# Rotary features: the exchanged halves come from the features by a product with a 0/1 matrix, instead of a second projection of the tokens

## The chip, the cores and the metric

The kernel runs on one core of a Trainium2 chip. A core has five engines with a queue each: TensorE (matrix products into PSUM, called PE in the profile; its weight loads are PEld), VectorE (DVE), ScalarE (ACT), GpSimd (POOL) and SyncE (SP, which here only issues transfers). Engines wait for each other through semaphores. The metric is the device time of one launch in microseconds, the median of three runs.

## What is computed

A tensor of 2 x 2048 tokens with 256 features goes through two layers. Layer 0 is a layer norm, a linear recurrence and a sign-weight projection. Layer 1 is a layer norm, then an ALiBi attention beside a block with RMS norm, rotary attention (16 query heads, 4 key/value heads of 16) and a mixture of 8 experts, 2 of them per token. The change touches how the rotary queries and keys are made:

```python
qkv = jnp.einsum('bsh,oh->bso', h, wqkv)          # h: RMS norm of the tokens
q = qkv[..., :NH * HD].reshape(B, S, NH, HD)      # 256 features
k = qkv[..., NH * HD:(NH + NKV) * HD]...          # 64 features
def _apply_rope(t, cos, sin):
    t1, t2 = jnp.split(t, 2, axis=-1)
    rot = jnp.concatenate([-t2, t1], axis=-1)     # halves of each head exchanged
    return t * cos[None, :, None, :] + rot * sin[None, :, None, :]
```

## The kernel before

The program has five stages in turn: `front` (layer norm and the recurrence's input), `middle` (projections), `attention` (both attentions), `after` (output projections and routing) and `experts`. The change is in `middle`; its weights are loaded in `front`, on SyncE's queue, and all transfers of weights are waited for by one count (`NW`).

`middle` works on eight blocks of 512 tokens (`NBLK = 8`, `BT = 512`), features on the partitions. Each engine has its own fixed list of work per block, the function `both(blk, more, ahead)`; `more` says that a next block exists, `ahead` that the block after next exists. Work on three blocks overlaps: in block blk, TensorE projects blk's tokens, turns u, xn and h of blk + 1 between them, and makes the first products (recurrence output with `c_mat`, sign weights) of blk + 2 (`first_products`).

TensorE's order in a block is: features 0 and 1 (ALiBi queries, from xT with `wa`), the turn of u, features 2 and 3 (keys), values 4 and 5, features 6 and 7, the turn of xn, features 8 and 9, the turn of h, features 10 and 11, the first products of blk + 2, values 12. Groups 6 to 12 come from hT with `wb`. `wb` holds the rotary weights, and beside them the same weights with the halves of each head exchanged: group 6 is query features 0 to 127, 7 the same with halves exchanged, 8 and 9 the other 128, 10 and 11 the 64 key features. A feature group is two accumulating products (the 256 inputs in two parts) into a PSUM bank; the banks 6, 7, 4, 5 go round (`BANK`). Products here are in float32 and appear as two records each. The turns are transposes with the identity matrix, eight records each.

ScalarE's order is: `scale_ffn(blk + 1)`, high parts 0 and 1, `deviation`, high parts 2 and 3, `squares(blk + 1)` (four sums of squares of xn, L704), `take_xT(blk + 1)` (two copies from PSUM and a small square root, L710 and L712), high parts 4 and 5 (L738), `take_hT(blk + 1)` (L717), high part 6. A high part is the result rounded to the narrower format that the attention reads; VectorE then forms the low part (L839), the rest.

VectorE's order is: `form_u(blk + 1)`, low parts 0 and 1, `add_residual`, low parts 2 and 3, `normalise` (makes xn), the values' bias, `mean_square(blk + 1)` (L813, waits for squares), `rope(4)`, `form_h(blk + 1)` (L817 and L820, waits for take_xT's square root), `rope(5)`, low parts 4 and 5, `rope(6)`, low part 6, and the copy of the rotary values (L889). `rope(m)` multiplies the group by cos (L850), its exchanged twin by sin (L851), and adds (L854).

The waits that tie them: the turn of h waits for `form_h`; `first_products(blk + 2)` waits until `take_xT` and `take_hT` of blk + 1 have emptied their banks; the next block's first features wait for the copy at L889.

Of the kernel before, what the change touches and what calls it, by code (L numbers as in the profile page):

```python
# [14 lines left out]
P = 128  # L15
# [3 lines left out]
TPB = 4  # L19
# [26 lines left out]
FT = FFN // P  # L46
SCALE = HD ** -0.5


# [22 lines left out]
def front(nc, A, M):  # L72
# [5 lines left out]
    with ExitStack() as ctx:  # L78
# [37 lines left out]
        s_aug, s_augr = sem("front_aug_loaded_then_stored"), sem("front_aug_rounded")  # L116
        x_d = A["x"].rearrange("b (n p) d -> p (b n) d", p=P)
        block = ctx.enter_context(nc.Block())

# [5 lines left out]
        def _(sp):  # L125
# [8 lines left out]
            for dst, src in ((M["wa"][:, :, :], A["w_qkv"].rearrange("(k p) m -> p k m", p=P)),  # L134
                             (M["bv"][:, :], A["b_qkv"][2 * D:3 * D].partition_broadcast(P)),
                             (M["wb"][:, :, :], A["w_b"].rearrange("(k p) m -> p k m", p=P)),
                             (M["cos"][:, :], A["c_cos"]), (M["sin"][:, :], A["c_sin"])):
                sp.dma_start(dst, src).then_inc(M["s_mid_weights"], 16)
# [249 lines left out]
def middle_weights(nc, ctx, M):  # L388

    for name, shape in (("c_mat", [P, D]), ("w_raw", [P, KD, D]), ("wa", [P, KD, 3 * D]), ("ba", [P, 4]),  # L390
                        ("bv", [P, D]), ("wb", [P, KD, 2 * D + 3 * KV * HD]), ("cos", [P, L]), ("sin", [P, L]),

                        ("cols", [P, KD, 4])):
        M[name] = ctx.enter_context(nc.sbuf_tensor("m_" + name, shape, F32))
    M["s_mid_weights"] = nc.alloc_semaphore("mid_weights_loaded")
    M["s_signs"], M["s_signed"] = nc.alloc_semaphore("signs_loaded"), nc.alloc_semaphore("signs_ready")
# [30 lines left out]
def middle(nc, A, M):  # L427

    with ExitStack() as ctx:
        def sb(name, shape, dt=F32):  # L430
            return ctx.enter_context(nc.sbuf_tensor(name, shape, dt))

        def sem(name):
            return nc.alloc_semaphore(name)
# [24 lines left out]
        NS = 7  # L459
        xf = [sb(f"m_xf{i}", [P, BT]) for i in range(2)]  # L460
        rots = [sb(f"m_rot{i}", [P, BT]) for i in range(2)]
# [12 lines left out]
        s_hi, s_xf, s_lo = sem("mid_high_part"), sem("mid_rope_ready"), sem("mid_low_part")  # L474
        s_va = sem("mid_v_ready")
        s_st = [sem(f"mid_rows_stored{s}") for s in range(2)]
# [7 lines left out]
        vb_d = M["vb_d"].rearrange("(n p) c -> p n c", p=P)  # L484
        NW = 10
        NDVE = 6
# [91 lines left out]
        def _(pe):  # L578
# [39 lines left out]
            def features(n, w, at, m, src):  # L618
# [4 lines left out]
                ins.then_inc(s_pr, 1)  # L623

            def values(n, w, at, m, src, tiles):

# [16 lines left out]
            def both(blk, more, ahead):  # L643
# [17 lines left out]
                pe.wait_ge(s_lo, blk * NS + 4)  # L661
                features(7, wb, D, P, hT)
                if more:
                    turn_xn(blk + 1)
                pe.wait_ge(s_pd, blk * NDVE + 2)
                features(8, wb, P, P, hT)
                pe.wait_ge(s_pd, blk * NDVE + 3)
                features(9, wb, D + P, P, hT)
                if more:
                    turn_h(blk + 1)  # L670
                pe.wait_ge(s_pd, blk * NDVE + 4)
                features(10, wb, 2 * D, KV * HD, hT)
                features(11, wb, 2 * D + KV * HD, KV * HD, hT)
                if ahead:
# [3 lines left out]
                    first_products(blk + 2)  # L678
                pe.wait_ge(s_pd, blk * NDVE + 5)
                values(12, wb, 2 * D + 2 * KV * HD, KV * HD, hT, range(TPB))  # L680

# [5 lines left out]
        def _(act):  # L687
# [36 lines left out]
            def both(blk, more, ahead):  # L724

                def high(m):
# [10 lines left out]
                    else:  # L737
                        sc.activation(part[m][0:n, 0, :], xf[(blk % 2 * NS + m) % 2][0:n, :], ACT.Copy).then_inc(s_hi, 1)  # L738

# [6 lines left out]
                high(2)  # L746
                high(3)
                if more:
                    squares(blk + 1)
                    take_xT(blk + 1)  # L750
                high(4)
                high(5)
# [7 lines left out]
        def _(dve):  # L760
# [66 lines left out]
            def both(blk, more, ahead):  # L827
                tok = blk % NBB * BT

                def low(m):  # L830
# [7 lines left out]
                    else:  # L838
                        ins = v.tensor_tensor(part[m][0:n, 1, :], xf[(blk % 2 * NS + m) % 2][0:n, :], high, ALU.subtract)  # L839
                    ins.then_inc(s_lo, 1)  # L840

                def rope(m):

                    rot = rots[m % 2]
                    i = (blk % 2 * NS + m) % 2
                    n = P if m < 6 else KV * HD
                    a, r = (6, 8, 10)[m - 4], (7, 9, 11)[m - 4]
                    dve.wait_ge(s_lo, blk * NS + (4 if m < 6 else 5))
                    dve.wait_ge(s_pr, blk * 13 + (r + 1))
                    ch.did(v.tensor_tensor(xf[i][0:n, :], ps[BANK[a % 4]][0:n, :], cos[0:n, tok:tok + BT], ALU.mult))  # L850
                    v.tensor_tensor(rot[0:n, :], ps[BANK[r % 4]][0:n, :], sin[0:n, tok:tok + BT],  # L851
# [1404 lines left out]
def constants():  # L2256
# [17 lines left out]
    ang = (np.arange(L, dtype=np.float32)[:, None] * inv[None, :]).astype(np.float32)  # L2274
    emb = np.concatenate([ang, ang], axis=1).T
    sign = np.where(np.arange(HD) < HD // 2, -1.0, 1.0).astype(np.float32)[:, None]
    c["c_cos"] = np.tile(np.cos(emb), (P // HD, 1)).astype(np.float32)
# [49 lines left out]
```

## Time and profile before

| | |
|---|---|
| median of 3 runs | 2570.25 us (2568.62 to 2571.12) |
| the profiled execution | 2568.78 us, with a span of 2566.9 us |
| TensorE busy | 2326.3 us, 91% of the span |
| VectorE, ScalarE, GpSimd busy | 1917.9, 1516.4 and 579.8 us |
| mean granted clock of TensorE | 0.964 |
| middle stage, from its first feature product to its last copy | 137.4 to 378.8 us |

The span is from the first to the last instruction. Busy time counts instructions of an engine; TensorE's products are pipelined, so that the length of one record is more than the distance to the next, and costs are better read from how far groups of records stand apart. The granted clock is a share of full speed: 1.00 is 2.4 GHz, 0.50 is 1.2 GHz.

### The profile page before, as it was taken

What the parts mean: (1) busy time and instruction counts of PE and PEld (TensorE: products, weight loads), DVE (VectorE), ACT (ScalarE), POOL (GpSimd) and SP (SyncE); (2) the same over time, 40 slices, a digit from 0 to 9 for tenths busy, and PEclk for the clock granted to TensorE, in tenths of its full rate; (3) what the DMA queues carried; (4) which work ended last, traced back from release to release, by engine and by line L of the source; (5) the groups of instructions that cost most, each with busy time, mean ns of one, the idle gap of its engine ahead of it and who ended that gap; (6) DMA issues with size and microseconds to landing.
All of it is one profiled execution on the core that took longest, in us unless ns stands there. A gap on an engine that the chain in (4) does not pass through costs nothing. (4 is left out here: it accounts for less than half of the span.)

```text
span 2566.9 us, 52951 instructions
## 1 busy us (share of the span) xinstructions
PE 2326.3 (91%) x18274; PEld 1266.1 (49%) x18275; DVE 1917.9 (75%) x4030; ACT 1516.4 (59%) x3290; POOL 579.8 (23%) x845
## 2 busy tenths in 40 slices
PE   3299987999999999999999999999999883999997
PEld 2155544444444444444444444444443662788886
DVE  6767758988998998999998999998993573233332
ACT  2033323677777787777787777777778461222221
POOL 4412101121111111111111111111000266423223
PEclk9599997999999999999999999999999996999999
DMA  4157766553443443322322322322020894343433
GB/s 156 62 161 207 222 193 98 86 104 76 72 77 73 78 78 67 70 56 46 66 54 52 64 53 55 63 48 61 31 78 26 284 299 186 64 77 76 78 74 70
DMA packets 168302, 246.55 MB, mean 96 GB/s; under 512 B 52392, under 2 KB 125240, under 8 KB 162244
## 3 DMA queue, kind: packets, MB, share of 16 engines
q0 software_dynamic: 38304, 112.51, 23.2%
q1 hardware_dynamic: 122404, 120.68, 15.9%
q10 hardware_dynamic: 7380, 10.48, 1.4%
q8 instruction: 138, 2.26, 0.4%
q14 instruction: 76, 0.62, 0.1%
HBM read 120.19 MB, written 122.36 MB: 94 GB/s over the span
## 5 line engine op out<-in xcount | busy, mean ns | idle before, releaser
L1411 DVE TENSOR_REDUCE a_mx<-banks 128x1 f32<-128x512 f32 (+3 forms) x2560 | 1378.5, 603 | 127.3 <-PE banks L1240 58.8
L1371 ACT ACTIVATE a_p<-banks 128x512 f32<-128x512 f32 (+3 forms) x2560 | 1177.6, 541 | 331.0 <-PE banks L1255 201.3
L1334 PE MATMUL banks<-a_p,a_v 128*32 128x512 f32 (+3 forms) x5120 | 597.8, 542 | 1.0 <-ACT a_p L1371 0.6
L1240 PE MATMUL banks<-a_k,a_q 48*128 48x512 f32 (+7 forms) x1600 | 340.4, 428 | 10.0 <-ACT a_p L1371 2.4
L1255 PE MATMUL banks<-a_q,a_k 50*128 50x512 f32 (+7 forms) x1600 | 332.3, 426 | 11.6 <-DVE a_mx L1411 4.4
L1240 PEld LDWEIGHTS banks<-a_k,a_q 52*128 52x128 f32 (+1 forms) x1600 | 154.6, 184 | 207.3 <-DVE a_mx L1411 164.2
L1255 PEld LDWEIGHTS banks<-a_q,a_k 54*128 54x128 f32 (+1 forms) x1600 | 152.3, 184 | 201.0 <-DVE a_mx L1411 144.9
L2103 ACT ACTIVATE e_hT<-banks 128x256 fp32r<-128x256 f32 x72 | 27.6, 383 | 308.5 <-PE banks L2029 278.9
L1240 PE MATMUL banks<-a_k,q 48*128 48x512 f32 (+7 forms) x896 | 191.5, 432 | 9.1 <-DMA a_k<-aug_rows 3.4
L2042 PE MATMUL banks<-w,e_hT 128*128 x576 | 184.1, 421 | 12.1 <-DVE e_hT L2143 12.1
L1255 PE MATMUL banks<-q,a_k 50*128 50x512 f32 (+7 forms) x896 | 186.3, 428 | 6.9 <-ACT a_p L1371 2.9
L2143 DVE TENSOR_TENSOR e_hT<-banks,e_hT 128x256 fp32r<-128x256 f32 x72 | 30.6, 425 | 196.3 <-ACT e_hT L2103 196.3
L2009 POOL DMA_INDIRECT out_rows<-e_y,e_token x72 | 111.6, 1550 | 250.9 <-DVE e_y L2163 202.6
L1334 PEld LDWEIGHTS banks<-a_p,a_v 128*32 128x32 f32 x5120 | 102.8, 108 | 113.6 <-issue 62.9
L1240 PEld LDWEIGHTS banks<-a_k,q 48*128 48x128 f32 (+1 forms) x896 | 87.6, 187 | 118.0 <-DVE a_mx L1411 92.0
L1255 PEld LDWEIGHTS banks<-q,a_k 50*128 50x128 f32 (+1 forms) x896 | 84.5, 184 | 122.3 <-DVE a_mx L1411 77.0
L2061 PE MATMUL banks<-w,e_gT 128*128 x576 | 136.5, 380 | 1.4 <-DVE e_y L2163 1.1
L2042 PEld LDWEIGHTS banks<-w,e_hT 128*128 128x128 f32 x576 | 109.6, 191 | 36.8 <-issue 13.4
L1225 PE MATMUL banks<-fill,before 64*128 64x64 bf16 x2048 | 124.7, 198 | 0.0
L1225 PE MATMUL banks<-fill,after 64*128 64x64 bf16 x2048 | 121.5, 197 | 0.0
L2061 PEld LDWEIGHTS banks<-w,e_gT 128*128 128x128 f32 x576 | 103.8, 190 | 13.4 <-issue 2.3
L1175 POOL DMA_DIRECT2D expert_rows<-a_zeros x132 | 98.6, 747 | 3.2 <-issue 3.2
(263 smaller groups left out, 2505.9 us busy)
## 6 DMA issues: line engine op xcount, KB each, us to landing
expert_rows<-a_zeros POOLq DMA_DIRECT2D x132, 258.0 KB, 5.2
a_k<-ka_parts POOLq DMA_DIRECT2D x42, 256.0 KB, 6.2
e_x<-expert_rows SPq DMA_DIRECT2D x72, 129.0 KB, 2.8
expert_rows<-e_y SPq DMA_DIRECT2D x72, 128.0 KB, 2.1
qa_parts<-m_part SPq DMA_DIRECT2D x16, 512.0 KB, 4.7
ka_parts<-m_part SPq DMA_DIRECT2D x16, 512.0 KB, 5.1
va_tiles<-m_va SPq DMA_DIRECT2D x8, 1024.0 KB, 5.0
qb_parts<-m_part SPq DMA_DIRECT2D x16, 512.0 KB, 4.7
```

The source lines that it names most:

```text
L1175: pool.dma_start(hs[:, i * FILL:(i + 1) * FILL, :], zeros[:, :, :]).then_inc(s_zs, 16)
L1225: ins = pe.matmul(outs[j][:, HALF * n:HALF * (n + 1)], steps[n][half, :], fill[half, :], start=False, stop=(n == 1))
L1240: ins = pe.matmul(outs[j][:, 0:w], q_op[o][part, p, qt * P:(qt + 1) * P], keys_of(r, k0)[part, kp, k0:k0 + w], start=True, stop=not diagonal)
L1255: ins = pe.matmul(outs[j][:, c0:QB], keys_of(r, kt * P)[part, kp, kt * P:(kt + 1) * P], q_op[o][part, p, qb * QB + c0:(qb + 1) * QB], star ...
L1334: ins = pe.matmul(ps_o[VW * h:VW * h + VW, c0:QB], v_op[o][:, kt, hk * VW:hk * VW + VW], prob[:, (n * GH + h) % NPB, c0:QB], start=(kt == ...
L1371: nc.scalar.activation(prob[:, (2 * n + j) % NPB, c0:QB], ps[(slot + j) % RING][:, c0:QB], ACT.Exp, scale=SCALE).then_inc(s_ex, 1)
L1411: v.tensor_reduce(mx[:, j, p, qt, k0 // WIDE:k0 // WIDE + 1], ps[banks[j]][:, 0:w], AX.X, ALU.max).then_inc(s_md, 1)
L2009: pool.indirect_dma_start(out=out, out_offset=bass.IndirectOffsetOnAxis(ap=token[n % R][:, :], axis=0), in_=y[n % R][:, :], in_offset=None ...
L2042: ins = pe.matmul(bank[:, :], hT[c][s][:, k, :], of[:, ds(at, 1), part * FFN:(part + 1) * FFN].rearrange("p o m -> p (o m)"), start=(k == ...
L2061: ins = pe.matmul(ps_y[:, 0:D], gT[s][:, f, :], w2[:, ds(e * FT + f, 1), :].rearrange("p o m -> p (o m)"), start=(f == 0), stop=(f == FT - 1))
L2103: nc.scalar.activation(hT[0][s][:, :, :].rearrange("p k t -> p (k t)"), ps_h[:, 0:D], ACT.Copy).then_inc(s_hi, 1)
L2143: v.tensor_tensor(hT[1][s][:, :, :].rearrange("p k t -> p (k t)"), ps_h[:, 0:D], high, ALU.subtract).then_inc(s_hT, 1)
```

## The change

`wb` keeps only the plain weights: query features, key features and values, which are loaded as three transfers (`WB_PARTS`). A 128 x 128 matrix of zeros and ones, `swap`, is loaded beside them; multiplied with 128 features it exchanges the halves of each head. ScalarE copies each rotary group from PSUM to `xf` (`copy(m)`, now three buffers), and TensorE multiplies `swap` with that copy (`swapped`), one product where there were two. The groups in TensorE's order are now: 6 (queries a), 7 (queries b), turn of xn, 8 (a exchanged), 9 (keys), turn of h, 10 (b exchanged), 11 (keys exchanged). VectorE's `rope` reads the group from `xf` instead of PSUM. In ScalarE's list, copies 4 and 5 come after high part 3 and ahead of `squares`, copy 6 after `take_xT`.

```diff
--- before.py
+++ after.py
@@ -47,6 +47,10 @@
 SCALE = HD ** -0.5
 
 
+
+WB_PARTS = ((0, 0, D), (D, 2 * D, KV * HD), (D + KV * HD, 2 * D + 2 * KV * HD, KV * HD))
+
+
 class Chain:
 
 
@@ -115,6 +119,7 @@
         s_step, s_pool, s_pw = sem("front_matrix_ready"), sem("front_pool"), sem("front_powers_ready")
         s_aug, s_augr = sem("front_aug_loaded_then_stored"), sem("front_aug_rounded")
         x_d = A["x"].rearrange("b (n p) d -> p (b n) d", p=P)
+        w_b = A["w_b"].rearrange("(k p) m -> p k m", p=P)
         block = ctx.enter_context(nc.Block())
 
         def vector_load(eng, dst, src, done):
@@ -133,7 +138,8 @@
                 sp.dma_start(dst, src).then_inc(M["s_signs"], 16)
             for dst, src in ((M["wa"][:, :, :], A["w_qkv"].rearrange("(k p) m -> p k m", p=P)),
                              (M["bv"][:, :], A["b_qkv"][2 * D:3 * D].partition_broadcast(P)),
-                             (M["wb"][:, :, :], A["w_b"].rearrange("(k p) m -> p k m", p=P)),
+                             *((M["wb"][:, :, to:to + m], w_b[:, :, of:of + m]) for to, of, m in WB_PARTS),
+                             (M["swap"][:, :], A["c_swap"]),
                              (M["cos"][:, :], A["c_cos"]), (M["sin"][:, :], A["c_sin"])):
                 sp.dma_start(dst, src).then_inc(M["s_mid_weights"], 16)
             sp.dma_start(aug[:, :], A["c_aug"]).then_inc(s_aug, 16)
@@ -388,7 +394,7 @@
 def middle_weights(nc, ctx, M):
 
     for name, shape in (("c_mat", [P, D]), ("w_raw", [P, KD, D]), ("wa", [P, KD, 3 * D]), ("ba", [P, 4]),
-                        ("bv", [P, D]), ("wb", [P, KD, 2 * D + 3 * KV * HD]), ("cos", [P, L]), ("sin", [P, L]),
+                        ("bv", [P, D]), ("wb", [P, KD, D + 2 * KV * HD]), ("swap", [P, P]), ("cos", [P, L]), ("sin", [P, L]),
 
                         ("cols", [P, KD, 4])):
         M[name] = ctx.enter_context(nc.sbuf_tensor("m_" + name, shape, F32))
@@ -457,7 +463,7 @@
         va = sb("m_va", [P, TPB, HEADS, VW])
         vb = sb("m_vb", [P, TPB, KV, VW])
         NS = 7
-        xf = [sb(f"m_xf{i}", [P, BT]) for i in range(2)]
+        xf = [sb(f"m_xf{i}", [P, BT]) for i in range(3)]
         rots = [sb(f"m_rot{i}", [P, BT]) for i in range(2)]
         part = [sb(f"m_part{m}", [P, 2, BT], F32R) for m in range(NS)]
 
@@ -472,7 +478,7 @@
         s_ht, s_hT = sem("mid_h_transposed"), sem("mid_hT_ready")
         s_pr, s_pd = sem("mid_projected"), sem("mid_taken_by_dve")
         s_hi, s_xf, s_lo = sem("mid_high_part"), sem("mid_rope_ready"), sem("mid_low_part")
-        s_va = sem("mid_v_ready")
+        s_va, s_cp = sem("mid_v_ready"), sem("mid_features_copied")
         s_st = [sem(f"mid_rows_stored{s}") for s in range(2)]
         s_pst, s_vst = M["s_moved"][:NS], M["s_moved"][NS]
         s_ms, s_rsd = sem("mid_mean_square"), sem("mid_rms_ready")
@@ -482,7 +488,7 @@
         xn_d = M["xn_d"].rearrange("(n p) d -> p n d", p=P)
         va_d = M["va_d"].rearrange("(n p) c -> p n c", p=P)
         vb_d = M["vb_d"].rearrange("(n p) c -> p n c", p=P)
-        NW = 10
+        NW = 13
         NDVE = 6
         BANK = [6, 7, 4, 5]
 
@@ -621,6 +627,13 @@
                     ins = pe.matmul(ps[BANK[n % 4]][0:m, :], w[:, c, at:at + m], src[:, c, :],
                                     start=(c == 0), stop=(c == KD - 1))
                 ins.then_inc(s_pr, 1)
+
+            def swapped(blk, n, m):
+
+                pe.wait_ge(s_cp, blk * 3 + (m - 3))
+                rows = P if m < 6 else KV * HD
+                pe.matmul(ps[BANK[n % 4]][0:rows, :], M["swap"][0:rows, 0:rows], xf[m - 4][0:rows, :],
+                          start=True, stop=True).then_inc(s_pr, 1)
 
             def values(n, w, at, m, src, tiles):
 
@@ -659,25 +672,24 @@
                 pe.wait_ge(s_lo, blk * NS + 3)
                 features(6, wb, 0, P, hT)
                 pe.wait_ge(s_lo, blk * NS + 4)
-                features(7, wb, D, P, hT)
+                features(7, wb, P, P, hT)
                 if more:
                     turn_xn(blk + 1)
                 pe.wait_ge(s_pd, blk * NDVE + 2)
-                features(8, wb, P, P, hT)
+                swapped(blk, 8, 4)
                 pe.wait_ge(s_pd, blk * NDVE + 3)
-                features(9, wb, D + P, P, hT)
+                features(9, wb, D, KV * HD, hT)
                 if more:
                     turn_h(blk + 1)
-                pe.wait_ge(s_pd, blk * NDVE + 4)
-                features(10, wb, 2 * D, KV * HD, hT)
-                features(11, wb, 2 * D + KV * HD, KV * HD, hT)
+                swapped(blk, 10, 5)
+                swapped(blk, 11, 6)
                 if ahead:
 
                     pe.wait_ge(s_xT, blk * KD + 2 * KD)
                     pe.wait_ge(s_hT, blk * KD + 2 * KD)
                     first_products(blk + 2)
-                pe.wait_ge(s_pd, blk * NDVE + 5)
-                values(12, wb, 2 * D + 2 * KV * HD, KV * HD, hT, range(TPB))
+                pe.wait_ge(s_pd, blk * NDVE + 4)
+                values(12, wb, D + KV * HD, KV * HD, hT, range(TPB))
 
             pe.wait_ge(s_w, NW * 16)
             pe.wait_ge(M["s_signed"], 1)
@@ -735,7 +747,16 @@
                         sc.activation(part[m][:, 0, :], ps[BANK[m]][:, :], ACT.Identity,
                                       bias=ba[:, m:m + 1]).then_inc(s_hi, 1)
                     else:
-                        sc.activation(part[m][0:n, 0, :], xf[(blk % 2 * NS + m) % 2][0:n, :], ACT.Copy).then_inc(s_hi, 1)
+                        sc.activation(part[m][0:n, 0, :], xf[m - 4][0:n, :], ACT.Copy).then_inc(s_hi, 1)
+
+                def copy(m):
+
+                    n = P if m < 6 else KV * HD
+                    a = (6, 7, 9)[m - 4]
+                    act.wait_ge(s_pr, blk * 13 + (a + 1))
+                    if blk >= 1:
+                        act.wait_ge(s_lo, (blk - 1) * NS + (m + 1))
+                    sc.activation(xf[m - 4][0:n, :], ps[BANK[a % 4]][0:n, :], ACT.Copy).then_inc(s_cp, 1)
 
                 if more:
                     scale_ffn(blk + 1)
@@ -745,9 +766,12 @@
                     deviation(blk + 1)
                 high(2)
                 high(3)
+                copy(4)
+                copy(5)
                 if more:
                     squares(blk + 1)
                     take_xT(blk + 1)
+                copy(6)
                 high(4)
                 high(5)
                 if more:
@@ -836,18 +860,18 @@
                         ins = v.scalar_tensor_tensor(part[m][:, 1, :], ps[BANK[m]][:, :], ba[:, m:m + 1], high,
                                                      ALU.add, ALU.subtract)
                     else:
-                        ins = v.tensor_tensor(part[m][0:n, 1, :], xf[(blk % 2 * NS + m) % 2][0:n, :], high, ALU.subtract)
+                        ins = v.tensor_tensor(part[m][0:n, 1, :], xf[m - 4][0:n, :], high, ALU.subtract)
                     ins.then_inc(s_lo, 1)
 
                 def rope(m):
 
                     rot = rots[m % 2]
-                    i = (blk % 2 * NS + m) % 2
+                    i = m - 4
                     n = P if m < 6 else KV * HD
-                    a, r = (6, 8, 10)[m - 4], (7, 9, 11)[m - 4]
+                    r = (8, 10, 11)[m - 4]
                     dve.wait_ge(s_lo, blk * NS + (4 if m < 6 else 5))
                     dve.wait_ge(s_pr, blk * 13 + (r + 1))
-                    ch.did(v.tensor_tensor(xf[i][0:n, :], ps[BANK[a % 4]][0:n, :], cos[0:n, tok:tok + BT], ALU.mult))
+                    ch.did(v.tensor_tensor(xf[i][0:n, :], xf[i][0:n, :], cos[0:n, tok:tok + BT], ALU.mult))
                     v.tensor_tensor(rot[0:n, :], ps[BANK[r % 4]][0:n, :], sin[0:n, tok:tok + BT],
                                     ALU.mult).then_inc(s_pd, 1)
                     dve.wait_ge(s_pd, blk * NDVE + m)
@@ -2273,6 +2297,7 @@
     inv = (1.0 / 10000.0 ** (np.arange(0, HD, 2, dtype=np.float32) / np.float32(HD))).astype(np.float32)
     ang = (np.arange(L, dtype=np.float32)[:, None] * inv[None, :]).astype(np.float32)
     emb = np.concatenate([ang, ang], axis=1).T
+    c["c_swap"] = np.eye(P, dtype=np.float32)[np.arange(P) // HD * HD + (np.arange(P) % HD + HD // 2) % HD]
     sign = np.where(np.arange(HD) < HD // 2, -1.0, 1.0).astype(np.float32)[:, None]
     c["c_cos"] = np.tile(np.cos(emb), (P // HD, 1)).astype(np.float32)
     c["c_sin"] = np.tile(np.sin(emb) * sign, (P // HD, 1)).astype(np.float32)
```

## Rows read from the trace of the kernel before

**Rows 1.** Stretches: length, busy PE, PEld, DVE, ACT, POOL, then granted clock, DMA, GB/s.
```profile
60.00:100.00 40.00, 0.00 (x0) 0.00 (x0) 38.46 (x82) 0.00 (x0) 15.58 (x19) 0.50 0.08 33
...
201.00:233.00 32.00, 31.39 (x111) 16.90 (x110) 23.55 (x52) 10.21 (x23) 5.40 (x5) 1.00 0.70 202
```

**Rows 2.** TensorE's timeline over that block; columns: start, length, what, times, idle before.
```profile
200.16 3.67 PE L621 MATMUL banks<-m_xT,m_wa 128*128 128x512 f32 x8 [0.61 <-DVE m_vb L889]
...
211.57 3.60 PE L621 MATMUL banks<-m_hT,m_wb 128*128 128x512 f32 x8
215.00 1.04 PE L606 MATMUL banks<-ident,m_xn 128*128 128x128 f32 x8
215.88 3.60 PE L621 MATMUL banks<-m_hT,m_wb 128*128 128x512 f32 x8
219.31 1.04 PE L614 MATMUL banks<-ident,m_h 128*128 128x128 f32 x8
220.28 3.65 PE L621 MATMUL banks<-m_hT,m_wb 128*64 128x512 f32 x8
223.86 1.98 PE L584 MATMUL banks<-f,m_c_mat 128*128 128x512 f32 x4
...
231.61 3.67 PE L621 MATMUL banks<-m_xT,m_wa 128*128 128x512 f32 x8 [0.61 <-DVE m_vb L889]
```

**Rows 3.** VectorE's timeline over the same block.
```profile
215.30 0.17 DVE L813 TENSOR_SCALAR m_msv<-m_ms 128x4 f32<-128x4 f32 x1 [0.45 <-ACT m_sq L704]
215.38 0.69 DVE L850 TENSOR_TENSOR m_xf<-banks,m_cos 128x512 f32<-128x512 f32 x1
...
216.70 0.69 DVE L854 TENSOR_TENSOR m_xf<-m_xf,m_rot 128x512 f32<-128x512 f32 x1
217.31 0.17 DVE L817 RECIPROCAL m_rs<-m_sd 128x4 f32<-128x4 f32 x1
217.52 1.14 DVE L820 TENSOR_SCALAR m_h<-m_xn,m_rs 128x256 f32<-128x256 f32 x4
219.58 0.69 DVE L850 TENSOR_TENSOR m_xf<-banks,m_cos 128x512 f32<-128x512 f32 x1 [0.92 <-PE banks L621]
```

**Rows 4.** ScalarE's timeline over the same block.
```profile
213.56 0.42 ACT L704 ACTIVATE m_sq<-m_xn 128x256 bf16<-128x256 f32 x1 [2.42 <-DVE m_xn L807]
...
215.08 0.19 ACT L704 ACTIVATION_READ_ACCUMULATOR m_sq<-m_xn 128x1 f32 x1
215.64 1.08 ACT L710 ACTIVATE m_xT<-banks 128x512 f32<-128x512 f32 x2 [0.37 <-PE banks L606]
...
221.63 0.63 ACT L738 ACTIVATE m_part<-m_xf 128x512 fp32r<-128x512 f32 x1 [3.58 <-DVE m_xf L854]
222.17 1.25 ACT L717 ACTIVATE m_hT<-banks,m_cols 128x512 f32<-128x512 f32 x2
```

**Rows 5.** VectorE's timeline, block 6.
```profile
350.08 0.68 DVE L850 TENSOR_TENSOR m_xf<-banks,m_cos 64x512 f32<-64x512 f32 x1 [1.05 <-PE banks L621]
```

**Rows 6.** TensorE's timeline, products after idle time at three places.
```profile
130.47 3.71 PE L584 MATMUL banks<-f,m_c_mat 128*128 128x512 f32 x4 [0.82 <-issue]
...
353.94 7.10 PE L621 MATMUL banks<-m_xT,m_wa 128*128 128x512 f32 x16 [2.04 <-DVE m_vb L889]
...
1989.80 3.65 PE L1661 MATMUL banks<-ident,t_rows 128*128 128x128 f32 x16 [3.37 <-PEq L989]
```

**Rows 7.** Busy time and granted clock (third column from the right) around idle stretches.
```profile
109.00:113.50 4.50, 0.02 (x1) 0.00 (x0) 4.43 (x6) 0.78 (x1) 4.32 (x4) 1.00 0.00 0
113.50:134.00 20.50, 9.44 (x28) 6.22 (x29) 9.64 (x24) 4.35 (x14) 6.99 (x6) 0.50 0.25 77
352.00:353.90 1.90, 0.00 (x0) 0.00 (x0) 1.10 (x3) 0.63 (x1) 0.00 (x0) 1.00 0.36 80
1986.40:1987.40 1.00, 0.03 (x1) 0.00 (x0) 0.68 (x2) 0.00 (x0) 0.00 (x0) 1.00 0.00 0
1987.40:1994.20 6.80, 4.40 (x19) 4.25 (x20) 0.00 (x0) 2.39 (x4) 0.66 (x2) 0.50 0.55 172
```

## The prediction

> **What bounds the kernel now.** I read the views in this order: busy time by stage, then the three engines' timelines over one block of the middle stage, then the places where TensorE stood idle and the clock granted around them.
>
> The change touches only the middle stage (eight blocks of 512 tokens, 137.4 to 378.8 us); front, attention and experts keep their instructions. In this stage TensorE is the bound: in one block it is busy 31.39 of 32.00 us at full clock, while VectorE has 23.55 and ScalarE 10.21 [rows 1]. The block that starts at 200.16 ends at 231.61, so the pitch is 31.45 us [rows 2]. TensorE runs one group straight after the other, and the only stall is 0.61 us at the block's end, for VectorE's copy of the last values [rows 2].
>
> I write times below as offsets from the block's first product (200.16 is 0). Before: features 6 and 7 run 11.41 to 14.84, the turn of xn to 15.72, features 8 and 9 to 19.15, the turn of h to 20.12, features 10 and 11 to 23.55, and the first products of the block after next start at 23.70 [rows 2]. Two chains on the other engines arrive just in time. ScalarE sums the squares at 13.40 (it had been idle 2.42 us, so it waits for VectorE alone), VectorE rotates features 4 from 15.22, form_h ends at 18.50, and the turn of h starts at 19.15, with only 0.65 us to spare [rows 2 to 4]. ScalarE's take_hT ends at 23.26, against 23.70 [rows 2, 4]: 0.4 us to spare. This lack of slack decides the case.
>
> **What it removes.** Eight records of a 128x512 product span 3.43 us, so a record costs 0.429 us and a feature group (two input halves, two records each) 1.716 us [rows 2]. A product with the exchange matrix has one input part, so 0.858 us. Three per block: 3 x 0.858 = 2.57 us less TensorE work, 8 x 2.57 = 20.6 us in all. The price of a 64-row exchange is bounded by 0 and 0.858; I take the latter, since the 64-column groups 10 and 11 cost as much as the 128-column ones [rows 2].
>
> **What it adds.** Three ScalarE copies from PSUM per block, at the price of take_xT: two take 1.08 us, 0.59 alone and 0.49 when another follows [rows 4]. VectorE's instructions stay as many; its first multiplication reads SBUF where it read PSUM, and both forms stand at 0.69 us [rows 3]: zero, bounds -0.1 and +0.1 each. The weight load becomes three transfers and a fourth brings the matrix, while the bytes shrink. They are issued in the front, and TensorE, the first to want them, has nothing to do from 60 to 100 us, while VectorE works through the recurrence [rows 1]: zero, bound +0.5.
>
> **Where the copies stand.** ScalarE works in its own order, and copies 4 and 5 are put ahead of the squares. Copy 5 cannot start before feature 7 has ended, at 14.84 + 0.27 = 15.11 (0.27 us is what lies between a group's end and its reader: features 8 and 9 end at 19.15, and VectorE reads at 19.42 [rows 2, 3]). The squares thus start at about 15.64 instead of 13.40. Following each queue on:
> - squares 15.64 to 17.35 (1.71 us, 213.56 to 215.27 [rows 4]); mean square on VectorE, then the rotation of 4 from 17.46, against 15.22 [rows 3]. The exchange 8 itself is ready at 15.72 + 0.86 + 0.27 = 16.85, so it isn't what ends the wait.
> - rotation 1.93 and reciprocal 0.21 (215.38, 217.31, 217.52), h 1.14 [rows 3]: h ready at 20.74, the turn of h starts at about 20.9.
> - TensorE meanwhile: exchange 8 to 16.58, feature 9 to 18.29, then idle to 20.9: **a first gap of 2.6 us**. The turn (0.97) ends at 21.85, exchange 10 at 22.71, exchange 11 at 23.57.
> - Here the second cost comes in. Before, the rotation of 5 began at 19.42 because its two halves were products 8 and 9, ahead of the turn of h. Now its exchanged half is product 10, behind that turn: it begins at 22.71 + 0.27 = 22.98. Its sum is there 2.01 us later; high part 5 takes ScalarE at 25.0, and take_hT, queued behind it (222.17 follows 221.63 by 0.54 [rows 4]), runs 25.57 to 26.82 (1.25 us).
> - first_products wait for both halves of hT, so they start at 26.9, not 23.57: **a second gap of 3.3 us**. From them to the next block's start it is 231.61 - 223.86 = 7.75 us [rows 2]: pitch 34.65, against 31.45.
>
> So the 2.57 us saved are gone and 3.2 us more: 6 blocks x 3.2 = +19.2 (blocks 0 to 5, which have first products behind them). Block 6 has none; its end is VectorE's. Its last rotation starts, after low part 5, at about 26.3 instead of 23.9 (350.08 in a block from 326.21) and the next block starts 3.86 us later (353.94) [rows 5, 6]: +2.4. In block 7 no turn stands between, the chain of rotations 5 and 6 starts at the same product end as before (feature 9's then, exchange 10's now, both at 17.3), and only rotation 6 no longer waits a moment for its product: an estimate of -0.2. Sum of the stall: **+21.4 us**.
>
> **The clock.** With such gaps TensorE may not keep its full clock. Rows (1.00 is the 2.4 GHz level, 0.50 the 1.2 GHz one): the idle stretch of 2.04 us ahead of the last block leaves it at 1.00; the one of 3.37 us, behind sparse work, finds it at 0.50 from 1987.4; idle from 109.0 it falls at 113.5 [rows 6, 7]. In the new block 2.6 us of idle, 0.97 of transposes, 1.7 of products and 3.3 of idle follow each other, which is more idleness than the first case and as much as the second. After work resumes it stays low for a while: at 130.47 until 134.0 (3.5 us), at 1989.80 until 1994.2 (4.4 us) [rows 6, 7]; four first products of 0.43 us each then take 3.71 [rows 6] instead of 1.98 [rows 2]. Work done at half clock loses half the time: 1.8 to 2.2 us per fall when it comes in the second gap, and about 1.3 more (turn 0.5 to 1, exchange 10 0.86) when it comes in the first. I take 2.6 per block between these, for seven blocks: **+18.2 us**. Bounds: 0, and 7 x 3.5 = 24.5.
>
> The Trainium skill (page "TensorE: Matmul & The Clock Gate", section "HAM oscillation — how this bites in real kernels") says that waits between bursts of matmuls send the clock back to its low level again and again, and counts the loss as half of the throttled time. By that rule the sum is the +39.6 below and not +21.4; the rows at 1987.4 and 113.5 agree, and no row shows a case of just these gaps.
>
> **Sum.** 21.4 + 18.2 = +39.6. The profiled execution has a span of 2566.9 and a time of 2568.8; its time becomes 2608.4. The median, 1.5 above it, goes from 2570.25 to **2609.9**.
>
> **Rivals.**
> - *Stall alone*: the gaps come, the clock stays full, as it does through the 2.04 us gap. Against it: the second gap is as long as the one at 1986.4. 2570.25 + 21.4 = 2591.7.
> - *Hidden (faster)*: the copies cost ScalarE nothing that anyone waits for. This needs the squares to start by about 14.0 and the rotation of 5 to end its high part before 21.5; ScalarE is only 32% busy in the block [rows 1], which speaks for it. Against it are the order of the queues and the end of feature 7. The point from which it decides: the slowdown is 3.2 us in a block, so the chain from feature 7 through both turns would have to be 3.2 us shorter than its rows to break even, 5.8 shorter for the full gain. Then 2570.25 - 20.6 = 2549.7.
> - *Break-even*: chains shorter by some 3 us, no fall of the clock: 2570.
> - *Deeper loss*: the clock falls in the first gap each time and transposes do not bring it back, 7 x 4.5 instead of 2.6 a block: 2623.
>
> **How the numbers follow.** Forecast 0.58, stall alone 0.24, deeper 0.08, hidden 0.07, break-even 0.03. The range goes from 2586 (stall alone less 6, if the chain is 0.9 us a block shorter) to 2624 (deeper); outside remain hidden, break-even and tails. 0.2% is 5 us, about what a measurement of this kernel can tell from no change. Faster by more: the hidden case, 0.07. Within: 0.03. Slower: 0.90.
>
> **What the profile after would show.** Right: block pitch of 34.6 us or more; exchange products 0.86 us each; ScalarE's first square 0.5 us behind copy 5; the turn of h idle before it for 2 to 3 us, released by VectorE's m_h; the first product with c_mat idle for 3 us or more, released by ScalarE's m_hT; granted clock below 1.00 between 137 and 400 us. Wrong: no idle time ahead of these two groups, a pitch of 28.9, or a clock of 1.00 throughout (stall alone). The prediction would fail if TensorE's queue ran exchange 10 ahead of the turn, or if the clock fell only in few blocks.

## The result, and the profile after

The changed kernel takes 2613.65 us (median of 4 runs, 2610.08 to 2614.76); beside it the kernel before takes 2570.68. The ratio is 1.0162, with a 95% interval of 1.0149 to 1.0174: 43 us slower. The profiled execution took 2614.76 us, with a span of 2612.8 against 2566.9.

The head of the page shows TensorE busy for 15 us more, although it has less to do:

```profile
PE 2341.4 (90%) x18226; PEld 1266.9 (48%) x18227; DVE 1916.0 (73%) x4030; ACT 1529.4 (59%) x3314; POOL 579.8 (22%) x845
```

The block of rows 2, now in the changed kernel, on TensorE (L620 is the turn of h, L635 the exchange products, L590 the first products' first group):

```profile
212.43 3.67 PE L627 MATMUL banks<-m_xT,m_wa 128*128 128x512 f32 x8 [0.61 <-DVE m_vb L913]
...
228.13 1.02 PE L635 MATMUL banks<-m_xf,m_swap 128*128 128x512 f32 x2
229.09 1.93 PE L627 MATMUL banks<-m_hT,m_wb 128*64 128x512 f32 x4
233.09 1.09 PE L620 MATMUL banks<-ident,m_h 128*128 128x128 f32 x8 [2.08 <-DVE m_h L844]
234.02 3.35 PE L635 MATMUL banks<-m_xf,m_swap 128*128 128x512 f32 x4
239.52 3.75 PE L590 MATMUL banks<-f,m_c_mat 128*128 128x512 f32 x4 [2.15 <-issue]
...
249.83 1.52 PE L627 MATMUL banks<-m_xT,m_wa 128*128 128x512 f32 x3 [0.61 <-DVE m_vb L913]
```

The block runs from 212.43 to 249.83, a pitch of 37.40 us where [rows 2] have 31.45. Two places matter. TensorE is idle for 2.08 us ahead of the turn of h, released by VectorE's m_h. And it is idle for 2.15 us ahead of the first products, which start at 239.52, although the four records of the exchange products before them have already taken 3.35 us (1.98 for four at the full clock in [rows 2]).

ScalarE in the same block (L759 the new copies, L716 squares, L722 take_xT, L750 a high part, L729 take_hT), to be held against [rows 4]:

```profile
227.46 0.60 ACT L759 ACTIVATE m_xf<-banks 128x512 f32<-128x512 f32 x1 [1.12 <-PE banks L627]
227.95 0.41 ACT L716 ACTIVATE m_sq<-m_xn 128x256 bf16<-128x256 f32 x1
...
237.63 0.63 ACT L750 ACTIVATE m_part<-m_xf 128x512 fp32r<-128x512 f32 x1 [5.20 <-DVE m_xf L878]
238.17 1.25 ACT L729 ACTIVATE m_hT<-banks,m_cols 128x512 f32<-128x512 f32 x2
```

Squares start 0.49 us behind copy 5, at 227.95, which is 15.52 in the block's own time; it was 13.40. take_hT sits right behind high part 5, which had waited 5.20 us; it ends at 238.17 + 1.25 = 239.42, and the first products start 0.10 us later. The profile names no releaser for them ("issue"); e2 below shows that it is take_hT.

VectorE (L837 mean square, L874 rotation, L844 form_h), to be held against [rows 3]:

```profile
229.68 0.17 DVE L837 TENSOR_SCALAR m_msv<-m_ms 128x4 f32<-128x4 f32 x1 [2.56 <-ACT m_sq L716]
229.75 0.69 DVE L874 TENSOR_TENSOR m_xf<-m_xf,m_cos 128x512 f32<-128x512 f32 x1
...
231.89 1.14 DVE L844 TENSOR_SCALAR m_h<-m_xn,m_rs 128x256 f32<-128x256 f32 x4
235.58 0.69 DVE L874 TENSOR_TENSOR m_xf<-m_xf,m_cos 128x512 f32<-128x512 f32 x1 [2.54 <-PE banks L635]
```

Mean square waits 2.56 us for the squares (0.45 before), rotation 5 waits 2.54 us for TensorE's exchange product (0.92 before).

Granted clock, the third column from the right, over this block, over its low stretch, and over the head of the attention stage, up to its first product with its own keys and queries (a_k, a_q):

```profile
core 0: us, PE busy (x) PEld busy (x) DVE busy (x) ACT busy (x) POOL busy (x), PEclk, DMA share, GB/s
212.43:249.83 37.40, 32.57 (x103) 16.38 (x103) 22.95 (x51) 11.76 (x26) 5.41 (x5) 0.86 0.58 168
234.48:244.72 10.24, 8.09 (x10) 2.46 (x9) 5.84 (x9) 2.41 (x4) 0.00 (x0) 0.50 0.48 126
...
423.22:524.26 101.04, 87.23 (x628) 41.23 (x628) 86.16 (x166) 42.87 (x90) 17.32 (x35) 0.69 0.60 97
```

The same head of the attention in the kernel before:

```profile
383.87:477.23 93.36, 77.94 (x628) 37.73 (x628) 84.95 (x165) 42.38 (x90) 17.29 (x35) 0.80 0.65 104
```

From 234.48 to 244.72 TensorE is at 0.50 (1.2 GHz): the clock falls behind the first gap and comes back in the first products. Eight low stretches, 58 us together, lie between block 0's start and 394.91, where the kernel before has none in its whole stage. They do not all begin in the same place. In blocks 0 to 2 the clock falls behind the first gap; in blocks 3 to 5 it holds through it and falls in the second. Block 3:

```profile
271.43 2.02 PE L635 MATMUL banks<-m_xf,m_swap 128*128 128x512 f32 x4
276.49 3.75 PE L590 MATMUL banks<-f,m_c_mat 128*128 128x512 f32 x4 [3.04 <-issue]
```

Here the exchange products run at the full clock, and the second gap shows its length, 3.04 us; the clock is at 0.50 from 275.44 to 282.27.

### The profile page after: what moved, and what is told of

It is laid out like the page before. It is cut to its first block and busy times, and to the rows that moved or that the text cites. A ratio compares the mean times of both kernels' runs of the same rounds, so it can differ in the third digit from the quotient of the medians.

```text
span 2612.8 us, 52911 instructions
## 1 busy us (share of the span) xinstructions
PE 2341.4 (90%) x18226; PEld 1266.9 (48%) x18227; DVE 1916.0 (73%) x4030; ACT 1529.4 (59%) x3314; POOL 579.8 (22%) x845
## 5 line engine op out<-in xcount | busy, mean ns | idle before, releaser
L2085 PE MATMUL banks<-w,e_gT 128*128 x576 | 136.5, 380 | 1.5 <-DVE e_y L2187 1.1
```

Source lines behind the costliest of these rows:

```text
L2085: ins = pe.matmul(ps_y[:, 0:D], gT[s][:, f, :], w2[:, ds(e * FT + f, 1), :].rearrange("p o m -> p (o m)"), start=(f == 0), stop=(f == FT - 1))
```

## Experiments

The first four kernels ran on one chip, beside a kernel before of 2570.74 us (15 runs). The last four ran on another, whose kernel before takes 2580.89 us (18 runs). In e6's profile the difference lies behind the attentions (587.5 us from there to the end, 577.1 in the profile before), not in the middle stage. Between the two chips only ratios, and stretches of the middle stage, are compared; the absolute times expected of the last four were meant for the first chip.

**e1: the gaps filled.**
```diff
                 if more:
+                    fill(BANK[2], 2)
                     turn_h(blk + 1)
...
                     pe.wait_ge(s_xT, blk * KD + 2 * KD)
+                    fill(0, 3)
                     pe.wait_ge(s_hT, blk * KD + 2 * KD)
...
+                if more and not ahead:
+                    pe.wait_ge(s_xT, blk * KD + 2 * KD)
+                    fill(0, 5)
```


> The changed kernel, with TensorE kept busy in the two gaps of each block by products of the exchange matrix with the cosines, into banks whose next product overwrites them: two records pairs (1.7 us) ahead of the turn of h, three pairs (2.6 us) ahead of the first products, five pairs in block 6. Nothing that any engine waits for is removed. Theory (the gaps cost their own length and, on top, the clock falls in them): block pitch 34.6 to 34.8 instead of 37.4, granted clock 1.00 through the stage, some 19 us faster than the changed kernel, 2592 to 2596. Rival (the pitch of 37.4 is all queueing, and the low clock only sits in idle time): no gain, or up to 5 us slower, 2613 or more.

Measured: 2591.22 us, ratio 1.0076 (1.0059 to 1.0093), 22.4 us faster than the changed kernel although TensorE does more. (`fill` multiplies `swap` with the cosines into a bank that the next product overwrites.) TensorE's timeline (L634 the fill) and the block's busy times and clock:

```profile
224.98 1.98 PE L634 MATMUL banks<-m_cos,m_swap 128*128 128x512 f32 x4
227.13 1.09 PE L620 MATMUL banks<-ident,m_h 128*128 128x128 f32 x8 [0.17 <-DVE m_h L854]
228.06 2.02 PE L640 MATMUL banks<-m_xf,m_swap 128*128 128x512 f32 x4
230.01 2.84 PE L634 MATMUL banks<-m_cos,m_swap 128*128 128x512 f32 x6
233.08 1.99 PE L590 MATMUL banks<-f,m_c_mat 128*128 128x512 f32 x4 [0.22 <-ACT m_hT L739]
```

```profile
206.46:240.84 34.38, 33.38 (x113) 17.10 (x113) 22.96 (x51) 11.77 (x26) 5.40 (x5) 1.00 0.64 183
```

The turn of h starts at 20.67 in the block (20.66 in the changed kernel), so the first gap's end is not moved; the clock is 1.00, and so it is through the whole stage; the pitch is 34.38. The clock alone is 37.40 - 34.38 = 3.0 us of this block; the queueing is 34.38 - 31.45 = 2.9. Of the gain, 19.3 us lie ahead of the attention's first product (403.91 against 423.22).

**e2: the second chain alone repaired.**
```diff
                 copy(6)
                 high(4)
-                high(5)
                 if more:
                     take_hT(blk + 1)
+                high(5)
                 high(6)
```


> The changed kernel, with take_hT ahead of high part 5 in ScalarE's list, nothing else. Theory (the second gap is take_hT queued behind high part 5, which waits for the exchange product behind the turn of h): the second gap vanishes, the first products follow the exchange products at once, the turn of h keeps its idle 2.1 us; pitch 31.3 if the clock stays, up to 33.5 where it still falls in the first gap; 2570 to 2585. Rival (first products wait for something else, or the first gap is the origin of both): pitch stays above 36, 2605 or more.

Measured: 2578.89 us, ratio 1.0034 (1.0021 to 1.0046). Two blocks on TensorE:

```profile
204.42 3.67 PE L627 MATMUL banks<-m_xT,m_wa 128*128 128x512 f32 x8 [0.61 <-DVE m_vb L913]
...
225.10 1.09 PE L620 MATMUL banks<-ident,m_h 128*128 128x128 f32 x8 [2.08 <-DVE m_h L844]
226.03 2.02 PE L635 MATMUL banks<-m_xf,m_swap 128*128 128x512 f32 x4
227.98 1.98 PE L590 MATMUL banks<-f,m_c_mat 128*128 128x512 f32 x4
...
235.74 3.67 PE L627 MATMUL banks<-m_xT,m_wa 128*128 128x512 f32 x8 [0.61 <-DVE m_vb L913]
...
256.42 1.09 PE L620 MATMUL banks<-ident,m_h 128*128 128x128 f32 x8 [2.08 <-DVE m_h L844]
257.35 3.63 PE L635 MATMUL banks<-m_xf,m_swap 128*128 128x512 f32 x4
...
270.36 1.95 PE L627 MATMUL banks<-m_xT,m_wa 128*128 128x512 f32 x4 [0.61 <-DVE m_vb L913]
```

No idle time is left ahead of the first products, and 2.08 us stay ahead of the turn of h. In the first of the two blocks the clock holds and the pitch is 31.32; in the second it falls, the exchange products take 3.63 us instead of 2.02, and the pitch is 34.62. The seven pitches are 34.44, 32.96, 31.32, 34.62, 32.95, 31.32 and 30.52. The expectation had 33.5 as the most; it is exceeded. The gap is 2.08 us in all seven blocks. At the full clock it leaves a pitch of 31.32, about that of the kernel before: it costs what the exchange products save. In two blocks (2 and 5) the clock holds through it, in the other five it falls right behind it, and that costs up to 3.3 us more. No run shows what decides between the two.

**e3: the copies alone, in the kernel before.** Three copies at the same places, into a tile that is dead by then, with the waits that their banks need; nobody reads them. The third copy takes product 8 instead of 9.
```diff
+                def copy(m):
+                    a = m + 2
+                    act.wait_ge(s_pr, blk * 13 + (a + 1))
+                    ...
+                    sc.activation(f[:, m % 2, :], ps[BANK[a % 4]][:, :], ACT.Copy).then_inc(s_cp, 1)
...
                 high(3)
+                copy(4)
+                copy(5)
                 if more:
                     squares(blk + 1)
                     take_xT(blk + 1)
+                copy(6)
                 high(4)
```


> The kernel before, with its second projections, and with three more copies from PSUM on ScalarE at the places where the changed kernel has them; nobody reads the copies. Theory (the first gap is the squares queued behind copy 5): the squares start at 15.6 instead of 13.4 in the block, the turn of h is idle for 1.6 us, pitch 33.1 instead of 31.45, clock at 1.00; 2582. Rival (the three copies are hidden because ScalarE is 32% busy, and the delay is due to the exchange products alone): 2570, pitch 31.45.

Measured: 2583.47 us, ratio 1.0043 (1.0026 to 1.0060).

```profile
203.57 3.67 PE L622 MATMUL banks<-m_xT,m_wa 128*128 128x512 f32 x8 [0.61 <-DVE m_vb L907]
...
224.27 1.09 PE L615 MATMUL banks<-ident,m_h 128*128 128x128 f32 x8 [1.39 <-DVE m_h L837]
...
236.63 1.96 PE L622 MATMUL banks<-m_xT,m_wa 128*128 128x512 f32 x4 [0.61 <-DVE m_vb L907]
```

```profile
219.11 0.41 ACT L707 ACTIVATE m_sq<-m_xn 128x256 bf16<-128x256 f32 x1
```

The squares (L707) start at 219.11 - 203.57 = 15.54 in the block, as in the changed kernel (15.52), so it is the copies that move them. Pitch 33.06, idle 1.39 us ahead of the turn of h (L615), at a clock of 1.00 over the block. ScalarE at a third of its time busy does not hide three copies of 0.6 us; their place in the queue costs 1.6 us a block.

**e4: the changed kernel in another order.**
```diff
-                copy(4)
-                copy(5)
                 if more:
                     squares(blk + 1)
+                copy(4)
+                if more:
                     take_xT(blk + 1)
+                copy(5)
                 copy(6)
-                high(4)
-                high(5)
                 if more:
                     take_hT(blk + 1)
+                high(4)
+                high(5)
                 high(6)
...
-                rope(4)
                 if more:
                     form_h(blk + 1)
+                rope(4)
                 rope(5)
```


> The changed kernel with its instructions in another order: on ScalarE squares, copy 4, take_xT, copies 5 and 6, take_hT, high parts 4, 5, 6; on VectorE form_h ahead of the rotation of 4. Same instructions. Theory (TensorE's 2.57 us per block are real and only queueing gave them back): no idle above 0.3 us ahead of the turn of h or the first products, pitch 28.8, full clock, 2549 to 2553. Rival (the exchange products are dearer than half a projection, or VectorE becomes the bound at a pitch near 31): 2565 to 2575.

Measured: 2558.97 us, ratio 0.9963 (0.9951 to 0.9974), faster than both kernels, but 6 us above the slow end of what was expected.

```profile
194.98 3.67 PE L627 MATMUL banks<-m_xT,m_wa 128*128 128x512 f32 x8 [0.61 <-DVE m_vb L914]
...
213.61 1.09 PE L620 MATMUL banks<-ident,m_h 128*128 128x128 f32 x8
214.54 2.02 PE L635 MATMUL banks<-m_xf,m_swap 128*128 128x512 f32 x4
216.49 1.98 PE L590 MATMUL banks<-f,m_c_mat 128*128 128x512 f32 x4
...
224.25 1.95 PE L627 MATMUL banks<-m_xT,m_wa 128*128 128x512 f32 x4 [0.61 <-DVE m_vb L914]
```

TensorE has no idle time but the 0.61 at the end, and the pitch is 29.27, 2.2 less than before instead of 2.57. Two exchange products in a row take 216.49 - 214.54 = 1.95 us, not 1.72. The other shortfall is at the end of the stage, first TensorE ahead of block 7, then VectorE (L875 rotation of 6, L914 the copy that block 7 waits for):

```profile
340.04 9.38 PE L627 MATMUL banks<-m_xT,m_wa 128*128 128x512 f32 x16 [4.36 <-DVE m_vb L914]
```

```profile
336.18 0.68 DVE L875 TENSOR_TENSOR m_xf<-m_xf,m_cos 64x512 f32<-64x512 f32 x1
...
339.48 0.41 DVE L914 COPY m_vb<-banks 128x256 f32<-128x256 f32 x1
```

TensorE is idle for 4.36 us and then takes 9.38 us, partly at the low clock, for 16 records (7.10 in [rows 6]). The pitch of block 6 is 27.77, as before (27.73): it ends with VectorE's copy, and faster products gain nothing. From block 0's start to the attention's first product e4 takes 372.29 - 136.60 = 235.7 us, the kernel before 383.87 - 137.45 = 246.4.

**e5: e4, with the copy of the rotary values (`take_vb`) earlier in block 6.**
```diff
-                pe.wait_ge(s_pd, blk * NDVE + 1)
+                pe.wait_ge(s_pd, blk * NDVE + (1 if more else 0))
...
+                early = more and not ahead
                 rope(4)
                 rope(5)
                 low(4)
+                if early:
+                    take_vb(6)
                 low(5)
                 rope(6)
                 low(6)
...
+                if not early:
+                    take_vb(7)
```


> The reordered kernel (e4), where in block 6 alone VectorE copies the rotary values out of their bank right after low part 4, ahead of low part 5 and the rotation of 6, and block 7's first features wait for that copy alone. Theory (in e4 TensorE stands idle 4.4 us ahead of block 7 because that copy is queued behind the rotation of 6, and the clock then falls): the idle time shrinks to under 1 us, the pitch of block 6 goes from 27.8 to 24.2, block 7's first features take 7.1 instead of 9.4 us; 5 to 6 us faster than e4, about 2553. Rival (block 7 is bound by VectorE's own chain, so an earlier start is given back): 2557 to 2560.

Measured: 2564.61 us beside 2580.89, ratio 0.9936 (0.9910 to 0.9961), the lowest of all. e4 had 0.9963 (0.9951 to 0.9974) on the other chip, and the two intervals overlap, so that the step from e4 rests on the trace.

```profile
312.21 3.67 PE L627 MATMUL banks<-m_xT,m_wa 128*128 128x512 f32 x8 [0.61 <-DVE m_vb L912]
...
336.23 7.10 PE L627 MATMUL banks<-m_xT,m_wa 128*128 128x512 f32 x16 [0.61 <-DVE m_vb L912]
```

Block 6 takes 24.02 us and block 7's first features 7.10, as expected; the attention begins at 366.21, against 372.29 in e4 and 383.87 in the kernel before. The place of the copy in VectorE's list was what held block 6. Block 7 gains nothing in any order: to the attention's first product it takes 366.21 - 336.23 = 29.98 us, in the kernel before 383.87 - 353.94 = 29.93.

**e6: the kernel before in e4's order.**
```diff
-                high(4)
-                high(5)
                 if more:
                     take_hT(blk + 1)
+                high(4)
+                high(5)
                 high(6)
...
-                rope(4)
                 if more:
                     form_h(blk + 1)
+                rope(4)
```


> The kernel before, with its second projections, in the order of e4: form_h ahead of the rotation of 4 on VectorE, take_hT ahead of high part 4 on ScalarE. Theory (TensorE is the bound of the kernel before, so order alone brings nothing and e4's gain is the exchange products'): pitch 31.3 to 31.5, 2569 to 2572. Rival (e4's 12 us come from the order): 2558 to 2562.

Measured: 2579.41 us beside 2580.89, ratio 0.9999 (0.9989 to 1.0008), pitch 31.45. No change is what was expected. The order alone gains nothing.

Block 7 of this run bears on the clock. The gap ahead of it is the same as in [rows 6], 2.04 us behind the same products, but here the clock falls in it (0.50 from 352.60 on), and the 16 records take 8.72 us where the kernel before has 7.10:

```profile
352.75 8.72 PE L621 MATMUL banks<-m_xT,m_wa 128*128 128x512 f32 x16 [2.04 <-DVE m_vb L889]
```

**e7: e4 with take_hT put back.**
```diff
-                if more:
-                    take_hT(blk + 1)
                 high(4)
                 high(5)
+                if more:
+                    take_hT(blk + 1)
                 high(6)
```


> e4 with one thing put back: take_hT behind high parts 4 and 5 on ScalarE, as in the changed kernel; the chain to the turn of h stays repaired. Theory (two causes, each with a gap of its own): no idle time ahead of the turn of h, but some 3 us ahead of the first products, pitch 32.4 at full clock and up to 34 with the clock falling in that gap; 2578 to 2588. Rival (the second gap is only the echo of the first): pitch 29.3, 2559.

Measured: 2599.02 us beside 2580.89, ratio 1.0067 (1.0041 to 1.0094), which on the first chip would be 2588, the slow end of what was expected.

```profile
204.80 3.67 PE L627 MATMUL banks<-m_xT,m_wa 128*128 128x512 f32 x8 [0.61 <-DVE m_vb L914]
...
223.42 1.09 PE L620 MATMUL banks<-ident,m_h 128*128 128x128 f32 x8
...
229.42 3.25 PE L590 MATMUL banks<-f,m_c_mat 128*128 128x512 f32 x4 [3.04 <-issue]
...
238.84 1.53 PE L627 MATMUL banks<-m_xT,m_wa 128*128 128x512 f32 x3 [0.61 <-DVE m_vb L914]
```

No idle time ahead of the turn of h; 3.04 us of it ahead of the first products; pitch 34.04, with part of the first products at the low clock. The second gap is not an echo of the first. The place of take_hT in ScalarE's list costs 34.04 - 29.27 = 4.8 us a block: 3.0 are the gap, and the rest is the clock (its mean is 0.95 in this block, and 0.05 x 34.04 is 1.7).

**e8: e4 with every exchange product twice.**
```diff
-                pe.matmul(ps[BANK[n % 4]][0:rows, :], M["swap"]..., xf[m - 4]..., start=True, stop=True).then_inc(s_pr, 1)
+                for _ in range(2):
+                    ins = pe.matmul(ps[BANK[n % 4]][0:rows, :], M["swap"]..., xf[m - 4]..., start=True, stop=True)
+                ins.then_inc(s_pr, 1)
```


> e4 with every exchange product issued twice into the same bank, the second overwriting the first. Theory (an exchange product costs TensorE 0.86 us and TensorE is e4's bound in blocks 0 to 5): pitch 31.8 instead of 29.26, 15 to 17 us slower than e4, 2574 to 2576, all of the change's saving given back. Rival (in e4 VectorE or ScalarE is the bound, TensorE has room): under 6 us slower, 2565 or less.

Measured: 2588.46 us beside 2580.89, ratio 1.0032 (1.0021 to 1.0043); against e4's 0.9963 that is 0.69%, or 18 us, where 15 to 17 were expected.

```profile
199.99 3.67 PE L627 MATMUL banks<-m_xT,m_wa 128*128 128x512 f32 x8 [0.61 <-DVE m_vb L916]
...
220.40 3.74 PE L636 MATMUL banks<-m_xf,m_swap 128*128 128x512 f32 x8
...
231.82 3.67 PE L627 MATMUL banks<-m_xT,m_wa 128*128 128x512 f32 x8 [0.61 <-DVE m_vb L916]
```

The pitch is 231.82 - 199.99 = 31.83, 2.56 more than e4's: 0.85 for each further product. In these blocks TensorE is e4's bound.

## Why the prediction was right

The forecast was 2609.9 us (+39.6), the measured median 2613.65 (+43.0), inside the range, and the likeliest case is the one that came: stall with falling clock. The mechanism is shown, step by step; that the sum is so close is in part luck, as the last items say. By its steps, in the block's own time:

- *Squares behind copy 5.* Forecast 15.64, measured 15.52. e3 shows it as a cause by itself: +1.6 us a block in a kernel that the exchange product is no part of.
- *The turn of h.* Forecast 20.9, measured 20.66 (233.09 - 212.43); feature 9 ends at 18.38 (four records from 16.66), so the gap is 2.3 us where 2.6 was forecast (the profile, with its modelled ends, calls it 2.08).
- *Rotation 5 behind the turn.* Forecast 22.98, measured 23.15; exchange product 10 was already slowed by the clock (in e1, at 1.00, it is 22.73). e7 shows this chain as a second cause.
- *First products.* Forecast 26.9, measured 27.09. The sign that was named, 3 us of idle time released by ScalarE's m_hT, came only in part: 2.15 us in this block, since the slowed exchange products fill the rest, 3.04 in block 3, and no releaser by name.
- *The clock.* Forecast 2.6 us a block. From block 0's start to block 7's the changed kernel takes 391.64 - 137.80 = 253.8 us, e1, with the fill and the full clock, 236.0, the kernel before 216.5 (353.94 - 137.45): queueing 19.5 (forecast 19.2 + 2.4 = 21.6, 2 us too much), clock 17.8. Block 7 adds 1.7 more, with its first 16 records at 8.73 us:

```profile
391.64 8.73 PE L627 MATMUL banks<-m_xT,m_wa 128*128 128x512 f32 x16 [4.19 <-DVE m_vb L913]
```

 The forecast of 18.2 for seven falls stands against 17.8 + 1.7 = 19.5, 1.3 us too little. Block by block, against e1's pitches, the clock costs 3.0, 3.0, 3.0, 2.9, 3.0, 1.4 and 1.5 us. So the price of a full fall was set too low, and the two cheap ones made up for it. The two cases that it was averaged from are wrong as well: 1.8 to 2.2 us for a fall in the second gap, 1.3 more for one in the first. Measured, both cost 3.0 (blocks 3 and 4, blocks 0 to 2). After a fall in the first gap the slower exchange products delay the first products by only 27.09 - 26.62 = 0.5 us beside e1, as TensorE would have waited there anyway; and the clock stays low over the first products and beyond them, 5.2 us of work in the block shown (239.52 to 244.72), where the rows had 3.5 and 4.4. What e1 cannot tell is whether the fill products also brought time by anything but the clock; that they do not move the turn's start speaks against it.
- *The whole stage.* The attention's first product starts at 423.22 instead of 383.87: +39.35, against +39.6. The 2 us too much in the queueing and what was missing from the clock cancel, and 0.35 of it is there before block 0 starts (137.80 instead of 137.45), inside the bound of 0.5 that the prediction gave the longer loading, and inside the scatter of the ten profiles, where block 0 starts between 136.5 and 137.9.

What the prediction left out lies behind the stage. The attention's head takes 101.04 us instead of 93.36 (rows above), at a mean clock of 0.69 instead of 0.80: +7.7. After it 1.1 us come back, so that the span is 45.9 longer. The prediction put everything behind the stage at nothing, because its instructions stay the same. The two profiled executions are 46.0 us apart, 6.4 more than forecast, and that is this head less what comes back; how the 3.4 us are made up by which the medians miss the forecast, no trace tells. That head is the same code in all ten kernels, and its length goes with how long it spends at the low clock:

| profile | low clock in the head, us | head, us |
|---|---|---|
| before | 36.9 | 93.4 |
| e8 | 39.4 | 93.3 |
| e4 | 40.6 | 94.5 |
| e2 | 40.8 | 94.5 |
| e1 | 42.3 | 95.3 |
| e6 | 46.8 | 96.0 |
| e3 | 47.1 | 95.9 |
| e5 | 50.1 | 97.0 |
| e7 | 57.5 | 97.6 |
| changed kernel | 63.5 | 101.0 |

That is about 0.26 us for each us at the low clock (a straight line through the ten). It is a correlation, not an experiment. Whether the longer low stretch of the changed kernel comes from when the stage starts, or is chance of that execution, stays open: its four runs spread over 4.7 us, and the trace is of the slowest.

The rivals: *stall alone* did not come, but e1 is that case, made by hand: 2591.22 where it forecast 2591.7, with a stage 19.6 us longer up to the attention's first product (403.91 - 137.88 = 266.0) where it had 21.4. *Hidden* is what e4 and e5 make of the same instructions. The full gain of 20.6 us that it named does not exist even there (e5's stage, 366.21 - 136.54 = 229.7 us, is 16.7 shorter than the 246.4 before), since two terms of it were too good: an exchange product that stands alone or in a pair costs 0.96 us to the next group's start (228.13 to 229.09) or 0.975 each (e4), and 0.85 only as a further one (e8), so that they save 2.2 us a block and not 2.57; and block 7 gains nothing (29.98 against 29.93). Block 6 gains only once VectorE's copy is moved (27.77 in e4, 24.02 in e5).

The four orders side by side, mean pitch of blocks 1 to 5: neither gap 29.3 (e4), first gap alone 32.6 (e2), second alone 34.1 (e7), both 37.0 (the changed kernel), both at full clock 34.4 (e1), and before 31.5. Without the clock the two gaps simply add up: the first alone raises 29.3 to 31.3 (e2, block 2), the second alone to about 32.3 (e7, an estimate: 34.04 less the 1.7 us of clock), and 29.3 + 2.0 + 3.0 is e1's 34.4 to within 0.1.

## What to carry to other kernels

Where each engine works down a list, an added instruction costs what is queued behind it, not its own 0.6 us: follow its wait to the next engine and on until it meets the bounding engine, and ask of each product that is moved behind another who is waiting for it: the rotation of 5 lost its early start because its exchanged half went behind the turn of h. A change that takes work off the bounding engine needs the other engines' lists laid out anew; here the same instructions give 1.0162 or 0.9936 of the time before. And idle time on TensorE can have a price beyond its length: in the block shown the pitch grew by 5.9 us, and 3.0 of that was the clock.

## What the runs showed that was not expected

A gap of 2.08 us, followed by transposes, lets the clock fall in some blocks and not in others (e2: pitches 31.32 and 34.62 in neighbouring blocks), while the prediction had only an idle stretch of 2.04 us that left it at full and one of 3.37 us that did not. The first of these rows was one case of two: the same stretch of 2.04 us, ahead of block 7, brings the clock down in e6 and not in the kernel before, so that it was weak evidence for the rival *stall alone*. And five products a block that nobody reads made a kernel 22 us faster (e1).
